# Batch 0 of a two-layer kernel in another order, with x loaded in eight transfers

## The reference, cut to what matters

```python
# x (8, 256, 1024) float32; 8 batches, each with its own mask (1024 x 1024, int 0/1) and adapter id
def layer0(x, coeff, mask, W, b):
    out  = einsum('bsi,oi->bso', x, W) + b
    diff = einsum('bsi,bio->bso', x, 2 * mask - 1)
    return out + diff * coeff[:, None, None]
def layer1(x, ids, W, b, A_all, B_all):              # rank 16, 32 adapters
    A, B = A_all[ids], B_all[ids]                    # (8, 16, 1024), (8, 1024, 16)
    h = einsum('bsd,brd->bsr', x, A)
    return einsum('bsd,od->bso', x, W) + b + einsum('bsr,bor->bso', h, B)
x = x + layer0(x, condB_coeff, mask, L0_W, L0_b)
x = x + layer1(x, ids, L1_W, L1_b, lora_A, lora_B)
```

## Time and profile before

| | us |
|---|---|
| median of 3 runs | 409.04 (408.07 to 409.2) |
| the profiled execution | 409.28 |
| its span | 407.5 |
| TensorE busy | 397.8 (98%) |
| VectorE busy | 290.6 (71%) |
| ScalarE busy | 183.2 (45%) |
| moved by DMA | 63.33 MB |

### The profile page before, as it was taken

One profiled execution on the slowest core, in us unless ns is written; L12 is line 12 of the kernel. 1 busy time (PEld: TensorE's weight loads), 2 busy tenths in 40 slices (PEclk: granted clock), 3 DMA queues, 4 the chain that ended last, 5 costly groups with the idle time before them and its releaser, 6 DMA issues.

```text
span 407.5 us, 6136 instructions
## 1 busy us (share of the span) xinstructions
PE 397.8 (98%) x2356; PEld 365.3 (90%) x2356; DVE 290.6 (71%) x375; ACT 183.2 (45%) x289; POOL 26.5 (7%) x43
## 2 busy tenths in 40 slices
PE   7999989999999999999999999999999999999995
PEld 5788878889999999999999999999999999999995
DVE  2578878866887688676887679675887679775523
ACT  3565645544435344354444444354345434353322
POOL 1234510000001000010001000010001000000000
PEclk9999999999999999999999999999999999999999
DMA  7999997159532892249622893339732693346002
GB/s 267 287 272 262 246 275 189 51 144 251 161 97 74 194 244 76 80 136 238 182 82 72 197 225 97 93 120 196 189 110 77 184 238 103 104 129 168 0 2 103
DMA packets 93488, 63.33 MB, mean 155 GB/s; under 512 B 3595, under 2 KB 90643, under 8 KB 93460
## 3 DMA queue, kind: packets, MB, share of 16 engines
q1 hardware_dynamic: 93298, 62.77, 59.2%
q10 hardware_dynamic: 162, 0.18, 0.1%
HBM read 51.39 MB, written 8.39 MB: 147 GB/s over the span
## 4 chain that ended last, share of the span: by engine, by line
PE 90%; DMA 5%; SPq 3%; issue 1%; DVE 1%; ACT 0%
PE ps L946 28%; PE ps L948 14%; PE ps L997 13%; PE ps L996 13%; PE ps L995 13%; PE ps L919 3%; DMA xraw<-in_x_dram 2%; PE ps L1018 2%; DMA xrows<-in_x_dram 2%; SPq L292 1%; PE ps L975 1%; PE ps L974 1%; PE ps L973 1%; DMA araw<-in_L_cond_lora_A_w_dram 1%; SPq L261 0%
## 5 line engine op out<-in xcount | busy, mean ns | idle before, releaser
L946 PE MATMUL ps<-xhl,whi 128*128 128x512 f32 x512 | 183.9, 397 | 0.1
L948 PE MATMUL ps<-xhl,wlo 128*128 128x256 f32 x512 | 143.2, 280 | 0.0
L946 PEld LDWEIGHTS ps<-xhl,whi 128*128 128x128 f32 x512 | 96.1, 188 | 19.6 <-issue 0.5
L997 PE MATMUL ps<-w1hi,yhl 128*128 128x344 f32 (+1 forms) x336 | 107.8, 321 | 0.0
L996 PE MATMUL ps<-w1lo,yhl 128*128 128x344 f32 (+1 forms) x336 | 107.6, 320 | 0.0
L995 PE MATMUL ps<-w1hi,yhl 128*128 128x344 f32 (+1 forms) x336 | 107.5, 320 | 0.0
L948 PEld LDWEIGHTS ps<-xhl,wlo 128*128 128x128 f32 x512 | 96.6, 189 | 0.4
L707 DVE SCALAR_TENSOR_TENSOR wlo<-wm,cs_minus,whi 128x1024 fp32r<-128x1024 f32 x62 | 80.0, 1291 | 20.7 <-ACT whi L487 20.7
L487 ACT ACTIVATE whi<-wm,cs_minus 128x1024 fp32r<-128x1024 f32 x62 | 71.5, 1153 | 39.7 <-DVE wm L700 39.7
L700 DVE SCALAR_TENSOR_TENSOR wm<-wm,cs_twice,w0t 128x1024 f32<-128x1024 int32 x62 | 80.1, 1291 | 3.9 <-DMA wm<-in_mask_Bx4096x_ik_dram 2.8
L527 ACT ACTIVATE ysum<-ps,b0col 128x256 f32<-128x256 f32 x64 | 30.4, 475 | 87.2 <-PE ps L948 87.0
(11 more groups left out here) (72 smaller groups left out, 234.2 us busy)
## 6 DMA issues: line engine op xcount, KB each, us to landing
wm<-in_mask_Bx4096x_ik_dram SPq DMA_DIRECT2D x64, 512.0 KB, 4.7
xraw<-in_x_dram SPq DMA_DIRECT2D x28, 256.0 KB, 6.3
w0raw<-in_L_cond_W_dram SPq DMA_DIRECT2D x8, 512.0 KB, 5.3
w1raw<-_L_cond_base_weight_dram SPq DMA_DIRECT2D x8, 512.0 KB, 7.7
out_dram<-zst SPq DMA_DIRECT2D x18, 172.0 KB, 2.0
bt<-bhl SPq DMA_DIRECT2D x48, 64.0 KB, 2.4
out_dram<-zst SPq DMA_DIRECT2D x8, 164.0 KB, 2.0
out_dram<-zst SPq DMA_DIRECT2D x7, 176.0 KB, 2.0
```

The costliest lines, as they stand in the source:

```text
L946: nc.tensor.matmul(ps[:, bank, :], whi[:, s, k, :], xhl[:, b % 2, k, :], start=(k == 0), stop=False, skip_group_check=True)
L948: op = nc.tensor.matmul(ps[:, bank, 0:S], wlo[:, s, k, :], xhl[:, b % 2, k, 0:S], start=False, stop=(k == KT - 1), skip_group_check=True)
L997: op = nc.tensor.matmul(dst, lo, w1hi[:, c, cols], start=False, stop=(c == KT - 1), skip_group_check=True)
```

## The change

- x of the next batch: eight transfers, one for each group of 32 rows, each over all 128 partitions (1 KB in each), in place of four transfers, one for each column quarter, over 32 partitions (8 KB in each). The content of `xraw` is the same. VectorE's wait counts 128 in place of 64 a batch.
- SyncE's order in batch 0: the names are read before W1 chunk 0 and W0 chunk 2, the gathers of A and B come in pairs among the loads of the slabs, x of batch 1 ahead of W0 chunk 7 and W1 chunk 5, masks 8 to 11 in another order.
- Chunk 0 on TensorE: `first_layer1` does hi x hi and lo x hi for k = 0 to 3, then W0 chunk 1's units, then k = 4 to 7, then all products with x's lo parts. Two idle products go, b0's transpose comes before x's.
- The orders of POOL, ScalarE, VectorE and TensorE in batch 0 are other ones throughout.
- At the end two products of chunk 62 are held back, not one.

```diff
-    HELD = ((1, 2),)
+    HELD = ((1, 1), (1, 2))
...
-                for a in range(4):
-                    src = x[b, :, a * S:(a + 1) * S].rearrange("(n q) f -> q n f", q=Q)
-                    sp.dma_start(xraw[a * Q:(a + 1) * Q, :, :], src).then_inc(x_in, 16)
+                for r in range(S // Q):
+                    src = x[b, r * Q:(r + 1) * Q, :].rearrange("q (a f) -> a q f", f=S)
+                    sp.dma_start(xraw[:, r, :], src).then_inc(x_in, 16)
...
             sp.wait_ge(ids_in, 16)
+            names = read_names(range(0, 4))
             load_w1(0)
-            names = read_names(range(0, 4))
+            names += read_names(range(4, 8))
             load_w0(2)
+            load_a(range(4, 6))
+            load_a(range(6, 8))
+            load_b1()
             load_w1(1)
-            names += read_names(range(4, 8))
             load_mask(2)
-            load_w0(4)
+            load_b(range(0, 2))
             load_w0(3)
-            load_b1()
-            load_a(range(0, 4))
             load_w1(2)
             load_mask(3)
-            load_a(range(4, 8))
+            load_a(range(0, 2))
+            load_a(range(2, 4))
+            load_w1(3)
+            load_w0(4)
+            load_b(range(2, 4))
+            load_b(range(4, 6))
+            load_mask(4)
+            load_b(range(6, 8))
             load_w0(5)
-            load_w0(6)
-            load_w1(3)
-            load_mask(4)
             load_w1(4)
-            load_b(range(0, 8))
             load_mask(5)
             move_bias()
+            load_w0(6)
+            load_x(1)
             load_w0(7)
             load_w1(5)
-            load_x(1)
             load_mask(6)
...
# VectorE, from make_y(3)
+            make_y(3)
             chunk_lo(4)
-            make_y(3)
             make_w(5)
+            y_parts_lo(3)
             split_lo("b", 0, 0)
-            y_parts_lo(3)
+            chunk_lo(5)
             split_lo("w1", 4, 0)
             split_lo("w1", 4, 1)
-            chunk_lo(5)
             make_y(4)
             turn_rows(1, 1)
+            y_parts_lo(4)
+            make_w(6)
             split_lo("b", 0, 1)
-            make_w(6)
...
# TensorE
+            def first_layer1(ks, low):
+                if ks[0] == 0 and not low:
+                    pe.wait_ge(first_lo, 1)
+                for k in ks:
+                    if k == TG and not low:
+                        pe.wait_ge(w_lo, 1)
+                    if k % TG == 0 and low:
+                        pe.wait_ge(x_lo, first_lo_split(ST - 1, k // TG))
+                    elif k % TG == 0:
+                        pe.wait_ge(x_hi, first_split(ST - 1, k // TG))
+                    if low:
+                        op = nc.tensor.matmul(ps[:, l1_bank(0), S:], whi[:, 0, k, :], xhl[:, 0, k, S:],
+                                              start=(k == 0), stop=(k == KT - 1), skip_group_check=True)
+                    else:
+                        nc.tensor.matmul(ps[:, l1_bank(0), 0:S], whi[:, 0, k, :], xhl[:, 0, k, 0:S], ...)
+                        nc.tensor.matmul(ps[:, l1_bank(0), 0:S], wlo[:, 0, k, :], xhl[:, 0, k, 0:S], ...)
...
             idle_products(2)
+            turn_b0()
             turn_unit("x", 0, 0)
             turn_unit("x", 0, 1)
-            idle_products(2)
-            turn_b0()
             turn_unit("x", 1, 0)
             turn_unit("x", 1, 1)
             idle_products(3)
-            layer1(0, range(0, 8))
+            first_layer1(range(0, 4), False)
             turn_unit("w0", 1, 0)
             turn_unit("w0", 1, 1)
+            first_layer1(range(4, 8), False)
+            first_layer1(range(0, 4), True)
+            first_layer1(range(4, 8), True)
             turn_unit("w1", 0, 0)
             turn_unit("w1", 0, 1)
             turn_unit("w0", 2, 0)
             turn_unit("w0", 2, 1)
-            turn_unit("w1", 1, 0)
             layer1(1, range(0, 2))
...
```

More of the change, by code:

```diff
@@ L951, in layer1 @@
                     op.then_inc(l1_done, 1)
+            def first_layer1(ks, low):
[12 more added lines that the diff above has]
+                    else:
+                        nc.tensor.matmul(ps[:, l1_bank(0), 0:S], whi[:, 0, k, :], xhl[:, 0, k, 0:S],
+                                         start=(k == 0), stop=False, skip_group_check=True)
+                        nc.tensor.matmul(ps[:, l1_bank(0), 0:S], wlo[:, 0, k, :], xhl[:, 0, k, 0:S],
+                                         start=False, stop=(k == KT - 1), skip_group_check=True)
+                if low and ks[-1] == KT - 1:
+                    op.then_inc(l1_done, 1)
             def adapter_h(n):
@@ L1073, in _ @@
-            first_layer2(1, 0, 0)
-            first_layer2(1, 1, 0)
-            first_layer2(1, 0, 1)
+            adapter_h(0)
+            first_layer2(1, 1, 1)
             turn_unit("w0", 4, 0)
             turn_unit("w0", 4, 1)
-            first_layer2(1, 1, 1)
+            adapter_h(1)
+            layer1(3, range(0, 2))
+            layer1(3, range(2, 4))
             turn_unit("w1", 3, 0)
-            layer1(3, range(0, 2))
-            adapter_h(0)
             turn_unit("w1", 3, 1)
-            adapter_h(1)
@@ L1084, in _ @@
-            layer1(3, range(2, 4))
             layer1(3, range(4, 6))
+            layer1(3, range(6, 8))
+            first_layer2(2, 0, 0)
             turn_unit("w0", 5, 0)
             turn_unit("w0", 5, 1)
-            layer1(3, range(6, 8))
-            first_layer2(2, 0, 0)
+            first_layer2(2, 1, 0)
+            first_layer2(2, 0, 1)
             turn_unit("b", 0, 0)
             turn_unit("w1", 4, 0)
+            adapter_h(2)
             layer1(4, range(0, 2))
-            adapter_h(2)
@@ L1094, in _ @@
             layer1(4, range(2, 4))
-            first_layer2(2, 0, 1)
             layer1(4, range(4, 6))
+            layer1(4, range(6, 8))
             turn_unit("w1", 4, 1)
-            first_layer2(2, 1, 0)
-            adapter_h(3)
-            turn_unit("w0", 6, 0)
-            layer1(4, range(6, 8))
-            turn_unit("w0", 6, 1)
             first_layer2(2, 1, 1)
             first_layer2(3, 0, 0)
+            turn_unit("w0", 6, 0)
+            turn_unit("w0", 6, 1)
+            layer1(5, range(0, 2))
@@ L1105, in _ @@
+            adapter_h(3)
+            layer1(5, range(2, 4))
             turn_unit("b", 0, 1)
-            layer1(5, range(0, 2))
             first_layer2(3, 1, 0)
             turn_unit("w1", 5, 0)
-            layer1(5, range(2, 4))
+            layer1(5, range(4, 6))
+            layer1(5, range(6, 8))
             first_layer2(3, 0, 1)
+            first_layer2(3, 1, 1)
+            adapter_h(4)
             turn_unit("w1", 5, 1)
-            layer1(5, range(4, 6))
-            first_layer2(3, 1, 1)
@@ L1114, in _ @@
-            layer1(5, range(6, 8))
             turn_unit("w0", 7, 0)
             first_layer2(4, 0, 0)
+            first_layer2(4, 1, 0)
+            first_layer2(4, 0, 1)
             turn_unit("w0", 7, 1)
-            adapter_h(4)
+            layer1(6, range(0, 2))
             turn_unit("w1", 6, 0)
-            layer1(6, range(0, 2))
-            first_layer2(4, 0, 1)
-            first_layer2(4, 1, 0)
+            turn_unit("w1", 6, 1)
+            first_layer2(4, 1, 1)
             layer1(6, range(2, 4))
+            first_layer2(5, 0, 0)
@@ L1124, in _ @@
             layer1(6, range(4, 6))
             layer1(6, range(6, 8))
-            first_layer2(4, 1, 1)
+            first_layer2(5, 1, 0)
             adapter_h(5)
-            first_layer2(5, 0, 0)
-            turn_unit("w1", 6, 1)
-            first_layer2(5, 1, 0)
-            layer1(7, range(0, 2))
-            turn_unit("w1", 7, 0)
-            layer1(7, range(2, 4))
             first_layer2(5, 0, 1)
             first_layer2(5, 1, 1)
+            layer1(7, range(0, 2))
+            layer1(7, range(2, 4))
@@ L1136, in _ @@
+            turn_unit("w1", 7, 0)
+            layer1(7, range(4, 6))
+            adapter_h(6)
+            layer1(7, range(6, 8))
+            first_layer2(6, 0, 0)
+            first_layer2(6, 0, 1)
             turn_unit("w1", 7, 1)
-            first_layer2(6, 0, 0)
-            layer1(7, range(4, 6))
-            layer1(7, range(6, 8))
             first_layer2(6, 1, 0)
-            adapter_h(6)
-            first_layer2(6, 0, 1)
+            first_layer2(6, 1, 1)
             layer1(8, range(0, 2))
```

112 lines of the change are left out of this document (57 added, 55 removed).

## The result

| | before | after |
|---|---|---|
| median of the runs, us | 409.12 (408.07 to 409.42) | 453.0 (452.59 to 453.67, 4 runs) |
| span of the profiled execution, us | 407.5 | 451.6 |
| mean granted clock over the span | 1.00 | 0.961 |

The ratio is 1.1079, 95% interval 1.1053 to 1.1105: 10.8% slower, 44 us. The forecast was 439.1. The time lies 1 us above the range and at the very top of the forecast's own range (428 to 453). The way in which it went slower is the one that was forecast, but for the clock, which had been put down as a rival with 6 in 100.

A forecast was written before the change was run, and what follows sets the result against it. TensorE, busy 397.8 of 407.5 us, was taken as the bound, with x just in time for VectorE beneath it. 409.28 - 3.7 - 0.24 + 5.2 + 28.8 = 439.3, or 439.1 against the median; range 404.3 to 452.

The forecast's parts named there:

- the forecast's own range: Whole kernel with x on four engines, from the bounds on packet price: 428 to 453 us around 439.1.
- the clock: TensorE in the x waits: its fall was left out of the sum, since idle stretches up to 1.3 us don't lower it.
- Count of engines: x's DMA transfers: engines follow the outermost count up to 16; the source's 4 gives four engines.
- Price of x: Steady batches: 256 packets at 48 ns make x 12.3 us; six TensorE waits of 4.8 us cost 28.8.
- 2.45 us in hand: Steady batches, chunk 13: TensorE's spare time before a later x from VectorE stops it.
- Batch 0: Reordering and chunk 0 save 3.7 us; W1 chunk 5, late behind x, costs a wait of 5.2.
- The start: Chunk 0 on TensorE: fewer fillers, earlier b0 transpose and hi products first save 1.0 us.
- the A wait: TensorE's 0.8 us wait in batch 0 for the A gathers, claimed to go.
- SyncE: Its eight x issues take 0.45 us each and don't hold x up; the masks behind go out 1.8 later.
- The end: Last chunk: a second held-back product lets the adapter turn and last store move 0.24 us earlier, bounds 0 and 0.31.
- the clock case: Rival: four engines and TensorE's clock falls in each wait, up to 43 us more, 482, or 461 for half; 6 in 100.

The follow-up runs named there:

- e5: The changed kernel with 20 unused filler products on TensorE ahead of the sixth chunk of batches 1 to 6; 443.48 us, ratio 1.0837.
- e1: The changed kernel with x loaded as before, in four transfers over 32 partitions each, the new orders kept; 406.6 us, ratio 0.9939.
- e7: e6 with VectorE's split of W1 chunk 2 moved ahead of `make_w(3)`; 406.99 us, ratio 0.9948.
- e4: The changed kernel with x's source walked scattered, outermost count 8 (x's pieces misplaced, for timing only); 407.12 us, ratio 0.9936.
- e3: The changed kernel with x's source walked in order, outermost count 128 (x's pieces misplaced, for timing only); 406.83 us, ratio 0.9942.
- e10: The changed kernel with only batch 1's x in eight new transfers, x of batches 2 to 7 in the four old ones; 412.85 us, ratio 1.0054.
- e6: e1 with b0's transpose and VectorE's copy of it put back behind x's first two units; 406.76 us, ratio 0.9935.

## Why the prediction was right or wrong

**Count of engines: right.** "The count of engines follows the outermost count": 4 closing packets with an outermost count of 4, 8 with 8, 16 with 128, and x's time 11.7, 6.0 and no wait. The Trainium skill ("DMA: Bandwidth & Descriptors", why a DMA increments its semaphore by 16) states it as the largest number up to 16 that divides both sides' outermost counts; the three packet counts agree.

**Price of x: right.** 12.3 us forecast, 11.7 measured; the six waits 28.8 forecast, 26.9 measured (3.9 to 5.5 each). That TensorE would have 2.45 us in hand held too: with 8 engines x is 1.1 later than before; VectorE waits 1.89 for it, TensorE not at all.

**The clock: wrong, and this is the step that failed.** In the sum the lower clock behind the waits stood at nothing. The forecast put it away with the sentence that idle stretches of up to 1.3 us don't lower it. That was true and said nothing of stretches of 4 to 5.5. The rival had 6 in 100 and a price of 21 to 43 us beyond the waits, a whole or half a chunk of 6.2 us each time. Both parts were off: in the profiled execution the clock fell at every one of the seven waits, inside three of them and just behind the other four, and came back after 3.5 to 6 us of products, so that little more than layer 1 of one chunk ran at half rate. That is 1.6 to 2.9 us a wait, 12.6 in six, and e5 gives 9.5 back. What the two levels cost could be read from the earlier trace rows; what was not known was whether a wait of 5 us brings the lower one, and that doubt deserved far more than 6 in 100. The Trainium skill ("TensorE: Matmul & The Clock Gate") says that an idle TensorE falls back to half clock; here the windows agree, 1.00 to 0.50 inside chunk 13's wait of 4.7.

**Batch 0: a loss as forecast, other in its parts.** Forecast: 3.7 won and 5.2 lost, 1.5 behind. Measured: 3.7 behind at chunk 11. The place was right (W1 chunk 5, 4.06 us instead of 5.2), but that the two lie so near is in part luck: the slab was in at 57.0 and through GpSimd at 57.5 (forecast 56.5), and TensorE asked for it at 53.5 (forecast 51.3). The missing part is the clock again: behind the wait the granted clock was 0.54 and 0.61 from 58 to 62 us, and the products from 57.60 to 61.72 took 4.1 us where e1's trace has 2.5: 1.6 lost. What was won is less than 3.7: 4.1 + 1.6 - 3.7 = 2.0 by the trace, and 2.5 by e1's ratio, the end included, against 3.9. Two terms account for it. The start gave 0.3 (17.52 for 17.82) and not 1.0, since the b0 row lands 0.3 behind x's first rows, and TensorE, which transposes it first, began x at 8.99 instead of 8.45. And the A wait, which was to go, was followed by a new one of 1.0 to 1.2 for W1's low part, behind `make_w(3)` on VectorE, which waits for mask 3 and is then drawn out while GpSimd works (e7). What stood behind VectorE's waits for masks was not looked at in the forecast.

**SyncE: right in effect, wrong in the size.** The eight issues of x were to take 0.45 each. They took 0.53 to 1.60, where e4 with 8 engines has 0.60 and e3 with 16 has 0.43 (medians). That the four engines' queues were full is a likely reason that no run tests:

```profile
L261 SPq DMA_DIRECT2D xraw<-in_x_dram x8: 529/1049/1602, 95.6 to 102.3; - x8
```

The masks behind went out from 103.9, 9.0 us after the mask ahead instead of 2.9 before, so not two microseconds late but six, and still TensorE never waited for one.

**The end: right in sign,** 0.14 for 0.24.

**The sum** was 30.1 over before. Missing in it are 13.6 in the steady batches (12.6 of half clock and 1.0 of waiting that the list doesn't count), 1.6 of half clock in batch 0, and winnings of 1.8 that didn't come (0.7 at the start, 1.0 at W1's low part, 0.1 at the end); the waits were 3.0 too long (28.8 for 26.9, 5.2 for 4.1). 30.1 + 13.6 + 1.6 + 1.8 - 3.0 = 44.1, by the spans 44.1. The range ended at 452 because the clock case was left out at its top, although the forecast's own top was 453: the range was cut inside the mechanism that it held for the likeliest.

## What to carry to other kernels

Read the outermost count of both sides of every transfer, the DRAM side too: packets of a queue less pieces give the engines that it really uses. Two kernels with the same bytes and tile forms (the changed one and e3) differ here by 46 us, and e4 puts that down to the count. Before costing a wait of several microseconds on TensorE, add what the next products cost at the lower level (here 1.6 to 2.9 us for waits of 3.9 to 5.5), and if the wait can't go, fill it. A transfer that a queue can hide stays free until it eats the last microsecond in hand: x at 4.9 and at 6.0 us cost nothing, at 11.7 it cost a tenth of the kernel.

The best version is e1 at 406.6 us, 0.6% under the kernel before. The eight transfers bring nothing over four even when they use all engines (e3, 406.8, not told apart from e1), since x came in time already. e3 itself can't be used, as its pieces of x lie in the wrong places, and no run has eight transfers on 16 engines with x where it belongs.

## What the runs showed of the hardware

- An engine moves a 1 KB packet in 42 ns when nothing else is under way (97 GB/s over four engines); with start and end it is 46 ns over a batch's x.
- In the changed kernel's trace six waits of 3.9 to 5.5 us and one of 4.1 each brought the granted clock to 0.50, three of the seven inside the wait and four just behind it; waits of up to 1.4 us in batch 0 left it at 1.00. In four of e10's ten executions the mean granted clock stayed at 1.00.
- A pass of VectorE that takes 1.28 us took up to 3.20 when it began during a pass of GpSimd over one partition (ten traces), and GpSimd's took 3.25 and 3.48 instead of 2.4 when VectorE began first (two traces).
- Eight issues with the same count of pieces took SyncE 0.43 us each with 16 engines, 0.60 with 8 and 1.05 with 4 (medians of batch 1; e3, e4, changed kernel).
- Identical starts (e6, e7) reach the upper level about 0.5 us apart, told by the durations; the granted clock reads 1.00 through both.
- Filler products that nobody reads made a kernel 9.5 us faster.
